# First norm's statistics two steps ahead of use, one power for both norms, elu in two operations, and tile counts by TensorE in a graph attention and mixture-of-experts kernel

## What is computed

```
def gnn(h, adj, W, a):
    Wh = h @ W
    e = Wh @ a[:D] + swapaxes(Wh @ a[D:], 1, 2)
    e = where(e > 0, e, 0.2 * e)
    e = where(adj > 0, e, -inf)
    return elu(softmax(e) @ Wh)

def ffn(x, Wg, bg, W1, b1, W2, b2):          # 8 experts, top 2
    scores = x @ Wg.T + bg
    top, idx = top_k(scores, 2)
    combine = sum(softmax(top)[..., None] * one_hot(idx, 8), axis=-2)
    for e in range(8):
        y = relu(x @ W1[e].T + b1[e]) @ W2[e].T + b2[e]
        out = out + combine[..., e:e + 1] * y
    return out

x = x + gnn(layernorm(x), adj, W, a)
x = x + ffn(layernorm(x), Wg, bg, W1, b1, W2, b2)
```

## Time and profile before

| | |
|---|---|
| median of 3 runs | 550.41 us (547.84 to 554.26) |
| the profiled execution's own time | 548.71 us |
| its span | 546.8 us |
| busy: TensorE, VectorE | 389.5 us (71%), 381.2 us (70%) |
| busy: ScalarE, GpSimd | 317.9 us (58%), 320.9 us (59%) |
| mean granted TensorE clock | 0.863 of full speed |

### The profile page before, as it was taken

How to read it: one execution, slowest core, us unless ns; L and a number is a source line. 1 busy time by engine, 2 the same in 40 slices (tenths; PEclk the granted TensorE clock), 3 DMA queues, 4 the chain that set the end, 5 groups by cost and what they waited for, 6 DMA issues and landing times.

```text
span 546.8 us, 9051 instructions
## 1 busy us (share of the span) xinstructions
PE 389.5 (71%) x1949; PEld 303.4 (55%) x1949; DVE 381.2 (70%) x1385; ACT 317.9 (58%) x724; POOL 320.9 (59%) x305
## 2 busy tenths in 40 slices
PE   3686868778777832029999999999999999930000
PEld 2564547555555621018888888888888887620000
DVE  5799888868887754607777777777777776540771
ACT  1576776767777746007777777777777777510000
POOL 1333787788787876723666666666666574553000
PEclk9889997979999855559999999999999999975555
DMA  5592233223322224522222233222222232202999
GB/s 142 162 355 62 76 96 89 82 87 92 114 84 86 83 83 125 201 63 60 77 82 77 82 83 92 82 83 77 77 82 77 77 85 70 75 29 71 290 292 298
DMA packets 67619, 60.17 MB, mean 110 GB/s; under 512 B 7632, under 2 KB 57168, under 8 KB 67344
## 3 DMA queue, kind: packets, MB, share of 16 engines
q1 hardware_dynamic: 58768, 41.73, 27.7%
q0 software_dynamic: 8832, 18.24, 10.0%
HBM read 27.01 MB, written 24.54 MB: 94 GB/s over the span
## 4 chain that ended last, share of the span: by engine, by line
PE 40%; POOL 20%; issue 13%; DVE 9%; DMA 7%; SPq 5%; ACT 2%; DVEq 1%; POOLq 0%; ACTq 0%
POOL expert_slots L443 12%; PE bank L962 5%; PE bank L963 5%; PE bank L966 5%; POOL moe_rows L456 5%; PE bank L979 5%; PE bank L976 5%; PE bank L977 5%; SPq L402 4%; DMA moe_rows<-ys,ysi 3%; PE bank L943 2%; POOL rstd L433 2%; PE bank L951 2%; PE bank L903 2%; PE bank L905 1%
## 5 line engine op out<-in xcount | busy, mean ns | idle before, releaser
L456 POOL DMA_INDIRECT moe_rows<-ys,ysi x148 | 159.2, 1075 | 105.1 <-DVE ysi L813 69.1
L443 POOL DMA_INDIRECT expert_slots<-rows,slot_i x128 | 130.5, 1020 | 39.1 <-issue 36.4
L565 ACT ACTIVATE yb<-bank,b_sb 128x512 f32<-128x512 f32 x36 | 24.9, 691 | 62.6 <-PE bank L979 62.6
L976 PE MATMUL bank<-hh,w_hi 128*128 128x512 f32 x144 | 60.2, 418 | 0.0
L962 PE MATMUL bank<-xh,w_hi 128*128 128x512 f32 x144 | 57.9, 402 | 0.8 <-ACT xh L548 0.8
L979 PE MATMUL bank<-hl,w_hi 128*128 128x512 f32 x144 | 57.6, 400 | 0.1
L963 PE MATMUL bank<-xh,w_lo 128*128 128x512 f32 x144 | 57.6, 400 | 0.0
L966 PE MATMUL bank<-xl,w_hi 128*128 128x512 f32 x144 | 57.5, 399 | 0.0
L977 PE MATMUL bank<-hh,w_lo 128*128 128x512 f32 x144 | 56.8, 395 | 0.0
L822 DVE CAST hh<-z 128x512 fp32r<-128x512 f32 x36 | 17.2, 478 | 48.3 <-ACT z L556 47.7
L560 ACT ACTIVATE hh<-bank,b_sb 128x512 fp32r<-128x512 f32 x72 | 50.0, 695 | 0.0
(11 more groups left out here) (126 smaller groups left out, 986.8 us busy)
## 6 DMA issues: line engine op xcount, KB each, us to landing
xs<-expert_slots SPq DMA_DIRECT2D x37, 260.0 KB, 2.8
rows<-xn SPq DMA_DIRECT2D x32, 256.0 KB
x_all<-x SPq DMA_DIRECT2D x16, 256.0 KB, 3.0
w_raw<-w_t SPq DMA_DIRECT2D x2, 2048.0 KB, 11.5
w_raw<-moe_rows SPq DMA_DIRECT2D x16, 256.0 KB, 5.1
w_hi<-moe_rows SPq DMA_DIRECT2D x16, 256.0 KB, 5.3
out<-x_all SPq DMA_DIRECT2D x16, 256.0 KB, 4.1
moe_rows<-ys,ysi POOLq DMA_INDIRECT x148, 2.4
```

Source lines behind the costliest of these rows:

```text
L443: nc.gpsimd.indirect_dma_start(out=slots, out_offset=bass.IndirectOffsetOnAxis(ap=slot_i[q][:, k * SUB + j:k * SUB + j + 1], axis=0), in_= ...
L456: nc.gpsimd.indirect_dma_start(out=moe_rows, out_offset=bass.IndirectOffsetOnAxis(ap=ysi[b][:, t:t + 1], axis=0), in_=ys[b][:, t, :], in_o ...
L565: nc.scalar.activation(yb[:, :], ps_y[:, :], ACT.Identity, bias=b2_sb[:, e:e + 1]).then_inc(yb_ok, 1)
L976: nc.tensor.matmul(ps_y[:, :], w2_hi[:, e, c, :], hh[:, c, :], start=c == 0, stop=False)
```

## The change

Four edits are made together, all in the first stage.

1. The first norm's statistics of groups 4 to 15 are no longer taken in batches of four groups. In step t, group gx + 4 (which is t + 2) gets its bn_stats at the head of VectorE's step, its bn_aggr behind those of gx, and its variance in the second half of var2. Batches remain for group 0 and groups 1 to 3.
2. The power of both norms is one operation of GpSimd over 8 values per partition (4 for gx from 12 on), into rstds. The mean is copied to mean1.
3. elu and the residual take two operations in place of three: min(hrelu + 1, hexp), and that minus 1 plus x_all; xr is gone.
4. The running count seen_b is gone. TensorE adds earlier tiles' counts into the rank with three products of chosen_b, and sums the group's counts with four; VectorE keeps the count after each group (count_f) and the base that is added to the next group's rank. The count's product after the steps is gone.

More of the change, by code:

```diff
@@ L143, in gnn_moe_kernel @@
         chosen_b = sb("chosen_b", [P, SUB, E], BF16)
-        seen_b = sb("seen_b", [P, SUB + 1, E], BF16)
+        base = sb("base", [P, SUB, E])
         rank = sb("rank", [P, SUB, E])
@@ L210, in gnn_moe_kernel @@
         stats2_ok = sem("stats2_ok")
+        mean1_ok = sem("mean1_ok")
         aggr1_ok = sem("aggr1_ok")
@@ L234, in gnn_moe_kernel @@
         hexp_ok = sem("hexp_ok")
-        xr_ok = sem("xr_ok")
         u_ok = sem("u_ok")
@@ L262, in gnn_moe_kernel @@
         slot_ok = sem("slot_ok")
-        count_ps = sem("count_ps")
+        base_ok = sem("base_ok")
         count_ok = sem("count_ok")
@@ L579, in _ @@
             nc.vector.tensor_copy(token_f[:, :, :], cst[:, C_TOKEN:C_PAD].rearrange("p (k s) -> p k s", k=2))
+            nc.vector.tensor_copy(base[:, :, :], cst[:, C_BASE:C_TOKEN].rearrange("p (t e) -> p t e", t=SUB)).then_inc(base_ok, 1)
             dve.wait_ge(start_ok, 1)
@@ L680, in step @@
                     dve.wait_ge(aggr2_ok, gx + 1)
-                    nc.vector.tensor_scalar(var2[:, :], mv2[:, :, 1], EPS, None, ALU.add).then_inc(var2_ok, 1)
-                if g0 is not None:
-                    if not later(t - 6):
-                        dve.wait_ge(rstd1_ok, 1 + sum(g0 >= batch.start for batch in BATCHES[1:]))
+                    last = nc.vector.tensor_scalar(var2[:, 0, :], mv2[:, :, 1], EPS, None, ALU.add)
[3 more added lines that the diff above has]
+                    if ahead(gx):
+                        nc.vector.tensor_copy(mean1[:, bass.ds(gx + AHEAD, 1), :].rearrange("p g s -> p (g s)"), mv3[:, :, 0]
+                                              ).then_inc(mean1_ok, 1)
+                if g0 is not None:
+                    if isinstance(g0, int) and g0 < AHEAD:
+                        dve.wait_ge(rstd1_ok, 1 + (g0 >= BATCHES[1].start))
+                        rstd_of, mean_of = rstd1[:, g0:g0 + 1, :], mv1[:, g0:g0 + 1, :, 0]
+                    else:
+                        dve.wait_ge(rstd2_ok, g0 - AHEAD + 1)
+                        dve.wait_ge(mean1_ok, g0 - AHEAD + 1)
+                        rstd_of, mean_of = rstds[:, bass.ds(g0 - AHEAD, 1), 1, :], mean1[:, bass.ds(g0, 1), :]
                     if later(g0):
@@ L701, in step @@
                     dve.wait_ge(logit_ok, gl + 1)
-                    if later(gl):
-                        dve.wait_ge(seen_ok, 5 * gl)
-                    nc.vector.tensor_copy(seen_b[:, 0, :], seen_b[:, SUB, :]).then_inc(seen_ok, 1)
-                if gl is not None:
+                    dve.sem_inc(met, 1)
                     for j in range(SUB):
@@ L728, in step @@
                     dve.wait_ge(chosen_ok, gl + 1)
+                    if later(gl):
+                        dve.wait_ge(rank_ps, gl)
                     nc.vector.tensor_tensor(chosen_b[:, :, :], chosen[:, 0, :, :], chosen[:, 1, :, :], ALU.add
@@ L935, in _ @@
             by_steps(pe, step)
-            pe.wait_ge(rank_ok, GROUPS)
-            nc.tensor.matmul(ps_count, ones_b[:, :], seen_b[:, SUB, :], start=True, stop=True).then_inc(count_ps, 1)
             bounds = block_bounds(pe)
```

46 lines of the change are left out of this document (25 added, 21 removed).

## The result

The changed kernel takes 553.89 us (median of 20 runs, 550.46 to 555.31), the kernel before 551.19 us (20 runs, 547.84 to 554.26): ratio 1.0045, interval 1.0026 to 1.0064, so 2.5 us slower. The profiled execution took 552.35 us with a span of 550.6, 3.6 and 3.8 us more than before. A median here is over all runs, a ratio over the fast ones, so the two can differ a little.

The account below looks back on a forecast made before the run. GpSimd's unbroken run was taken to bound the first stage, TensorE the second. Terms -2.9 (start), +6.2 (power) and 0 (clashes) gave +3.3 us, 553.7 us on the median's footing; range 548.2 to 559.5.

Parts of the forecast that it names:

- the two large terms: First stage: GpSimd's unbroken run starts 2.9 us earlier, and its ten longer powers add 6.2 us.
- The bound: First stage after 52.40 us: runs at GpSimd's pace, 11.55 us a step, 12.2 us after the change.
- E: Rival, first stage: VectorE becomes the bound, one more microsecond for ten steps, +10, 563.7 us; chance 0.06.
- The start: Ahead of GpSimd's run: 13.5 us of statistics leave VectorE, mostly covered; run starts about 2.9 us earlier, at 49.5.
- The power: GpSimd's run: pow over 8 values instead of 4 takes 0.62 us more, ten times, +6.2 us on the path.
- the third: Traced pow of 16 values, 3.27 us; less a 0.39 us stall taken as 2.88, giving slope 0.153 us a value.
- The clashes: GpSimd's run: scatters that hit busy VectorE, 0.41 us a step, taken as unchanged; ends -5 to +5 us.
- C: Rival, GpSimd's run: back-to-back u, x_all, score always catch one or two scatters; sum +9.0, 559.4 us; chance 0.17.
- the sum: Whole kernel: start -2.9, power +6.2, clashes 0, together +3.3 us.

Follow-up runs that it names:

- four kernels of the first chip: The kernel before with edits 1 and 2 alone (ratio 1.0035), edit 3 alone (1.0019), edit 4 alone (0.9919), or statistics of groups 4 to 15 left out (0.9902).
- the batches left out: The kernel before without statistics and powers of groups 4 to 15, normed with group 3's mean and variance: 543.60 us, ratio 0.9902.

## Why the prediction was right

553.7 us was forecast, 553.89 measured. That they agree to 0.2 us is luck: the forecast was 3.3 us on top of a median of three runs, 550.41; over 20 runs the kernel before has 551.19, and the change costs 2.7 us by the medians, 2.5 by the ratio. The path and the two large terms were right, and the rest nets out. By its own steps:

The bound. GpSimd's pace held before and after, and in all four kernels of the first chip. In each of their 78 steps of the run, thirteen a kernel, the step less its power less its excess is 10.02 to 10.07 us, while VectorE's busy time from 52 to 200 us goes from 114.5 (after) and 115.3 (edit 4) over 119.5 (before) to 126.6 us (edits 1 and 2). So the pace followed the power and the excess alone. E is refuted by the 27.1 us for which VectorE stands.

The start. Forecast 2.9 us, measured 2.62; a later adjacency load (mask_b at 5.6 us, 5.4 before) had taken 0.2 of it. Step by step: score forecast at 46.0, found at 46.42; run forecast at 49.5, found at 49.78. What score waits for was wrong: the prediction has it 0.15 us behind z, at 45.85; z was there at 45.75, and score stood 0.67 us more behind u and x_all, now two operations of 0.69 us between hexp and score. With the batches left out the gain was 3.7 us: the worth of 13.5 us of VectorE was a quarter. With edits 1 and 2 alone it was 1.3 us, so that the 2.9 us can't be called shown for the statistics by themselves.

The power. Forecast 0.62 more each, measured 0.66; the line through the two undisturbed sizes was right, and so was the stall taken out of the third: in the kernel with edit 3 alone, and again in that with edits 3 and 4, two of the three powers of 16 values took 2.90 us, where I had 2.88.

The clashes. Taken as unchanged, measured +1.4 us over thirteen steps, between the ends of -5 and +5. The places were right within 0.2 us: u 2.2, x_all 3.0 and score 3.8 us from the power's end, and in the nine steps from 62.07 to 173.01 the fourth scatter starts in score every time (1.29 at 79.87: score ends at 80.32, less 79.87, less 0.12 is 0.33). In the changed kernel 20 scatters of the run start with more than 0.12 us left of u (8) or score (12), none of them in x_all, and each pays up to the operation's end less 0.12, within 0.01 us; 30 start inside bn_stats or xn, and none pays over 0.02. (In the kernel before and in three of the first chip's a few that start inside xn are 0.05 to 0.07 us longer.) So C's mechanism is there, at a quarter of its price: 1.4 us of 5.7.

What nets out: the run is 6.6 + 1.4 us longer by powers and clashes, and 1.2 shorter behind its last power, where fewer scatters met the splitting of the weights (w_lo on VectorE, 0.68 us each: three scatters, 1.6 us in all, before; one, 0.32 us, after). The last scatter is 4.2 us later, where the sum had 3.3, and the median 2.7. Neither the +1.4 nor the -1.2 was in the sum.

What I had not asked is the sign of each part: edits 1 and 2 cost 0.35%, edit 4 gains 0.8%, and the whole is worse than the product of the parts (0.997). The excess of 0.57 in the whole against 0.31 and 0.32 in the parts would be worth 13 x 0.25 = 3.3 us, 0.6%, about the difference. That edit 3 is what brings it is argued, not shown: no pair of edits was timed at the higher clock, and each excess is that of one execution.

## What to carry to other kernels

Ask of each piece of work that is moved which engine has idle time there: statistics were taken from a place where they were three quarters covered, and their power was put from an idle engine onto the one that sets the pace. When an engine runs without a gap, forecast the ends of its run, not the busy shares of the others. And where an operation of one engine holds up the start of another's, as here, ask where in the step it falls as well as how long it is.

## What the runs showed of the hardware

What a scatter pays for a VectorE operation with two inputs is decided at its start, within a tenth of a microsecond. At 92.82, above, the scatter started 0.07 us ahead of x_all and paid nothing, and x_all was not longer either. Close to the operation's start it goes either way: with edits 1 and 2 a scatter 0.01 us behind the start of x_all paid nothing, and x_all took 0.73 us; in the changed kernel one 0.03 us behind the start of u paid 0.54. The same step can so cost 0.06 or 0.6 us, and it can lock: six steps of 11.82 to 11.87 us in a row in the kernel with edits 1 and 2.

Once the GpSimd operation ran, neither engine waited for the other here. In the kernel with edit 3 alone u, x_all and score, two inputs each, run one after the other inside a power of 16 values, and all four have their undisturbed length; the power that began at 34.16, 0.09 us behind the start of such a u, took 3.37 us.

```profile
47.29 2.90 POOL L421 TENSOR_TENSOR rstd<-var,minus_half 128x16 f32<-128x16 f32 x1 [7.69 <-DVE var L605]
...
47.51 0.68 DVE L629 SCALAR_TENSOR_TENSOR u<-hrelu,hexp 128x512 f32<-128x512 f32 x1
48.22 0.69 DVE L634 SCALAR_TENSOR_TENSOR x_all<-u,x_all 128x512 f32<-128x512 f32 x1
48.96 0.68 DVE L652 SCALAR_TENSOR_TENSOR score<-z 128x512 f32<-128x512 f32 x1
```

The same program took 551 or 612 to 616 us by the chip. In the changed kernel without edit 3, on one of the slower, the chain of a step in the first stage reads so:

```profile
99.55 1.03 ACT hexp L520 x4
100.58 5.38 another core or an unknown queue
```

and the step's busy times, with a granted clock of 0.60:

```profile
93.00:110.40 17.40, 11.85 (x56) 9.34 (x57) 10.23 (x58) 8.27 (x27) 9.07 (x9) 0.60 0.20 62
```

Every engine is idle for 5.5 us of the step or more. The 5.4 us in which ScalarE stands for z, with TensorE's products for it recorded as done at 101.55, are put down to no engine. Most of the loss lies in this stage: the last scatter is at 290.0 us, 54 us later than in the kernel before above, and 323.1 us follow it in place of 310.7. Which comes first, the lower clock or the longer step, these runs don't tell.
